# Moving the first projection of batches 1 to 3 into the first attention, half a tile at a time

## The reference

```
qkv    = x @ qkv_w.T                                  (q, k, v per head)
scores = alpha * tanh(q k^T / beta) + lam/2 * s s^T + lat
         s = tanh(x @ hex_w.T),  h = tanh(x @ q6_w.T),  lat[head] = h M[head] h^T / 6 * scale
out    = softmax(causal(scores)) @ v
```

## Time and profile before

| | us |
|---|---|
| median of 3 runs | 4202.61 (4201.70 to 4206.91) |
| the profiled execution | 4210.31 |
| its span | 4208.5 |
| PE / ACT / DVE / POOL busy in it | 3719.3 / 3380.6 / 2746.0 / 455.1 |
| mean granted TensorE clock | 0.974 |

### The profile page before, as it was taken

One profiled execution on the slowest core, in us unless ns is written; L12 is line 12 of the kernel. 1 busy time (PEld: TensorE's weight loads), 2 busy tenths in 40 slices (PEclk: granted clock), 3 DMA queues, 4 the chain that ended last, 5 costly groups with the idle time before them and its releaser, 6 DMA issues. The chain is left out here.

```text
span 4208.5 us, 61509 instructions
## 1 busy us (share of the span) xinstructions
PE 3719.3 (88%) x21948; PEld 1426.6 (34%) x21958; DVE 2746.0 (65%) x4740; ACT 3380.6 (80%) x2758; POOL 455.1 (11%) x407
## 2 busy tenths in 40 slices
PE   6969999998998999999997858759999999999687
PEld 2432322322332322232232644422222222222565
DVE  5647888778888777888877878952323233232688
ACT  2439999999999999999998113439999999999233
POOL 3530000000000000000000216730000000000232
PEclk9989999999999999999999989979999999999899
DMA  5861111111112111211110535652212222221331
GB/s 163 257 208 56 48 57 54 45 40 57 59 47 60 45 45 46 60 48 58 54 45 15 165 122 153 190 162 69 80 58 81 68 74 77 69 81 38 112 91 50
DMA packets 281330, 348.02 MB, mean 83 GB/s; under 512 B 39310, under 2 KB 214510, under 8 KB 280753
## 3 DMA queue, kind: packets, MB, share of 16 engines
q1 hardware_dynamic: 281012, 343.97, 27.2%
HBM read 215.56 MB, written 128.25 MB: 82 GB/s over the span
## 5 line engine op out<-in xcount | busy, mean ns | idle before, releaser
L842 DVE SCALAR_TENSOR_TENSOR att_prob<-att_tanh,alpha,ps 128x512 f32<-128x512 f32 x2176 | 1506.5, 740 | 410.4 <-ACT att_tanh L786 367.4
L726 PE MATMUL ps<-att_q,att_k 99*128 99x512 bf16 (+5 forms) x5120 | 1135.0, 351 | 114.1 <-DMA att_v<-v_ones 56.3
L755 PE MATMUL ps<-att_prob,att_v 128*32 128x512 f32 (+3 forms) x10240 | 1162.4, 540 | 2.0 <-ACT att_prob L795 1.9
L786 ACT ACTIVATE att_tanh<-ps,rbeta 128x2048 f32<-128x2048 f32 x544 | 1125.6, 2069 | 35.8 <-PE ps L726 35.8
L795 ACT ACTIVATE att_prob<-att_prob 128x2048 f32<-128x2048 f32 x544 | 1095.6, 2014 | 1.5 <-DVE att_prob L842 1.3
L792 ACT ACTIVATE att_prob<-ps 128x1024 f32<-128x1024 f32 x1088 | 1054.3, 1021 | 25.9 <-PE ps L726 10.0
L736 PE MATMUL ps<-att_f,att_g 75*128 75x512 bf16 (+3 forms) x2560 | 810.9, 354 | 133.1 <-DVE att_prob L842 121.3
L726 PEld LDWEIGHTS ps<-att_q,att_k 96*128 96x128 bf16 (+1 forms) x5120 | 399.4, 98 | 962.7 <-ACT att_prob L792 428.1
L831 DVE TENSOR_TENSOR att_prob<-att_prob,keep 128x512 f32<-128x512 f32 (+1 forms) x320 | 187.4, 586 | 580.3 <-ACT att_prob L792 579.1
L736 PEld LDWEIGHTS ps<-att_f,att_g 75*128 75x128 bf16 x2560 | 231.7, 97 | 927.6 <-DVE att_prob L842 906.8
L755 PEld LDWEIGHTS ps<-att_prob,att_v 128*32 128x32 f32 x10240 | 216.1, 108 | 347.9 <-ACT att_prob L792 141.6
(11 more groups left out here) (130 smaller groups left out, 2450.6 us busy)
## 6 DMA issues: line engine op xcount, KB each, us to landing
v_ones<-proj_vs SPq DMA_DIRECT2D x128, 256.0 KB, 3.3
att_v<-v_ones SPq DMA_DIRECT2D x128, 256.0 KB
att_k<-k_parts SPq DMA_DIRECT2D x128, 192.0 KB
att_q<-q_parts SPq DMA_DIRECT2D x128, 192.0 KB
att_k<-k_parts SPq DMA_DIRECT2D x128, 128.0 KB
att_q<-q_parts SPq DMA_DIRECT2D x128, 128.0 KB
o_t<-att_on SPq DMA_DIRECT2D x512, 32.0 KB, 1.7
post_o<-o_t SPq DMA_DIRECT2D x32, 512.0 KB, 5.1
```

The source lines that it names most:

```text
L726: mm = pe.matmul(ps[:, bank, col:col + w], keys, q_s[:, n % QU, h, q0:q0 + w], start=True, stop=True)
L755: mm = pe.matmul(ps[VW * h:VW * (h + 1), O0 + n % 2, q0:q0 + w], v_s[:, c % KU, kb % CB, h * VW:(h + 1) * VW], prob[:, S % R, h, col:col + ...
L786: th.done(act.activation(tanh_s[:, S % 2], ps[:, QK0:QK0 + HQ], ACT.Tanh, scale=kn["rbeta"][:, 0:1]))
L842: sc.done(dve.scalar_tensor_tensor(prob[:, S % R, h], tanh_s[:, S % 2, h], kn["alpha"][:, 0:1], ps[:, E0 + h % 2], ALU.mult, ALU.add))
```

## The change

`project_phase(0)` runs over the four groups of batch 0 only. The other twelve groups `X` are made inside `attend_phase(0)`, one per set in sets 0 to 11. A group is nine *units*: g, q0, q1, k0, k1, f0, f1 and two halves of v. A unit is two *halves* on PE (one for an f). `slots` names the 16 steps of a set behind which a half is put. The unit goes into bank 6 or 7, whichever is free between two query groups. DVE copies q, k, f and v units out in the step after (g goes through ACT's tanh), between the second and the third sum. POOL makes all three parts with four operations, and SP stores them. Normalising moves ahead of the first sum. SP's order in the attention is written out by step, with the waits for the stores of a batch (`projected`) ahead of the loads that need them. `row_max_phase` gets the missing tiles in its flagged branch, which isn't run in the profile.

```diff
+    kinds = tiles + [("v", 0), ("v", 1)]
+    NX = (B - 1) * GB if layer == 0 else 0
+    slots = {7: (0, 0), 8: (0, 1), 12: (1, 0), 13: (1, 1), 14: (2, 0), 15: (2, 1), 16: (3, 0), 17: (3, 1), 18: (4, 0), 19: (4, 1),
+             24: (5, 0), 25: (6, 0), 26: (7, 0), 27: (7, 1), 28: (8, 0), 29: (8, 1)}
+    bank_of = {u: O0 + (1 if 1 <= u <= 4 else 0) for u in range(NU)}
+    behind = {0: 0, 1: 1, 5: 2}
+    ahead = {2: 0, 3: 4, 0: 8}
...
 @block.sync
+            for n in range(QU):
+                load(n)
+                if layer == 0 and n == 0:
+                    for name, t in (("wq", wq_s), ("wk", wk_s), ("wv", wv_s), ("w12", w12_s)):
+                        sp.dma_start(t[:], w[name]).then_inc(w_in, 16)
+                    load_x(0)
+                    load_x(1)
+            for S in range(N + 8):
+                if 4 <= S < N + 4:
+                    it, s, *_ = at(S - 4)
+                    for g in ends[s]:
+                        n = it * GB + g
+                        if n + QU < NG:
+                            o_tr.wait(sp, n)
+                            b = (n + QU) // (GB * NHQ)
+                            if layer == 0 and b > 0 and (n + QU) // GB % NHQ == 0:
+                                projected((b - 1) * GB + (n + QU) % GB)
+                            load(n + QU)
+                if 5 <= S < N + 5 and unit_at(S - 5) is not None:
+                    store_unit(unit_at(S - 5))
+                if 7 <= S < N + 7:
+                    it, s, *_ = at(S - 7)
+                    for g in ends[s]:
+                        store_o(it * GB + g)
...
 @block.tensor
+            def project(j, half):
+                X, kind, m, tile, n, bank = unit(j)
+                if half == 0:
+                    if j == 0:
+                        pe.wait_ge(w_in, 64)
+                    if kind == "g":
+                        pe.wait_ge(x_in[X % 2], 16 * (X // 2 + 1))
+                    bg_ev.wait(pe, j - 1)
+                    if j % NU in behind:
+                        o_tr.wait(pe, X * GB + behind[j % NU])
+                if kind == "f":
+                    mm = pe.matmul(ps[0:n, bank], kn["Cq"][:].rearrange("p q e h -> p (q e h)")[:, m * n:(m + 1) * n], f12[:, X % 2], start=True, stop=True)
+                elif kind == "v":
+                    at_t = slice((2 * m + half) * P, (2 * m + half + 1) * P)
+                    for c in range(DC):
+                        mm = pe.matmul(ps[:, bank, half * D:(half + 1) * D], xt_s[:, X % 2, c, at_t], wv_s[:, c, :], start=c == 0, stop=c == DC - 1)
+                else:
+                    lhs = w12_s[:, half, :] if kind == "g" else (wq_s if kind == "q" else wk_s)[:, half, m * P:(m + 1) * P]
+                    mm = pe.matmul(ps[0:n, bank], lhs, xt_s[:, X % 2, half], start=half == 0, stop=half == 1)
+                if half == 1 or kind == "f":
+                    bg_ps.done(mm)
...
                 if layer == 0 and S < N:
                     extra(S, 2)
                     extra(S, 3)
+                if half_at(S):
+                    project(*half_at(S))
...
 @block.scalar
+                if S > 0 and unit_at(S - 1) is not None:
+                    feature(unit_at(S - 1))
                 if S > 0 and layer == 0:
                     sc.wait(act, (S - 1) * HQ + HQ - 1)
...
 @block.vector
+            dve.memset(vs[:], 1.0).then_inc(ones_set, 1)
+            def evict(j):
+                if kind == "v":
+                    bg_ps.wait(dve, j)
+                    v_out.wait(dve, m, X - 1)
+                    bg_ev.done(dve.tensor_copy(vs[:, m, :, :, 0:HD], ps[:, bank].rearrange("p (t h d) -> p t h d", t=2, h=H)))
+                elif kind != "g":
+                    bg_ps.wait(dve, j)
+                    low.wait(dve, tile - 2)
+                    bg_ev.done(dve.tensor_copy(raw[0:n, tile % 2], ps[0:n, bank]))
...
-                    if h == 2:
+                    if h == 0:
                         normalise(due, 1)
+                    if h == 2 and S > 0 and unit_at(S - 1) is not None:
+                        evict(unit_at(S - 1))
                     th.wait(dve, S)
                     ex.wait(dve, S * HQ + h)
...
 @block.gpsimd
+                for j in range(NX * NU):
+                    bg_ev.wait(pool, j)
+                    parts_out.wait(pool, u, tile // 2 - 1)
+                    hi.done(pool.tensor_copy(parts[0:n, u, 0], src))
+                    rest.done(pool.tensor_tensor(rem[0:n], src, parts[0:n, u, 0], ALU.subtract))
+                    mid.done(pool.tensor_copy(parts[0:n, u, 1], rem[0:n]))
+                    low.done(pool.tensor_tensor(parts[0:n, u, 2], rem[0:n], parts[0:n, u, 1], ALU.subtract))
...
-        project_phase(nc, kn, 0, {"wq": chunked(a["wq0"]), "wk": chunked(a["wk0"]), "wv": chunked(a["wv0"]), "w12": chunked(a["w12"]), "xt": chunked(a["x0_t"])}, None)
+        project_phase(nc, kn, 0, w0, None, NB=1)
```

More of the change, by code:

```diff
@@ L628, in attend_phase, with half_at, unit_at, unit @@
     QK0, E0, O0 = 0, 4, 6
+    tiles = [("g", 0), ("q", 0), ("q", 1), ("k", 0), ("k", 1), ("f", 0), ("f", 1)]
+    NTL = len(tiles)
+    kinds = tiles + [("v", 0), ("v", 1)]
+    NU = len(kinds)
+    NX = (B - 1) * GB if layer == 0 else 0
[4 more added lines that the diff above has]
+    ahead = {2: 0, 3: 4, 0: 8}
+    def half_at(S):
+        it, s = divmod(S, NST)
+        if it >= NX or s not in slots:
+            return None
+        return it * NU + slots[s][0], slots[s][1]
+    def unit_at(S):
+        found = half_at(S)
+        return found[0] if found and (found[1] == 1 or unit(found[0])[1] == "f") else None
+    def unit(j):
+        X, u = divmod(j, NU)
+        kind, m = kinds[u]
+        return X, kind, m, X * NTL + u, {"q": P, "k": P, "f": 96, "g": NF, "v": P}[kind], bank_of[u]
     SR, FR = (QROWS, FROWS + 3) if layer == 0 else (QROWS + 3, 0)
@@ L753, in weigh @@
                         o_tr.wait(pe, n - 2)
+                        X = it - 1 if g == 0 else it
+                        if g in ahead and 0 <= X < NX:
+                            bg_ev.wait(pe, X * NU + ahead[g])
                     for h in range(HQ):
@@ L779, in _, with feature @@
                 c.start(act)
+            def feature(j):
+                X, kind, m, tile, n, bank = unit(j)
+                if kind == "g":
+                    bg_ps.wait(act, j)
+                    if X >= 2:
+                        low.wait(act, tile - 2 * NTL)
+                    bg_ev.done(act.activation(f12[:, X % 2], ps[0:NF, bank], ACT.Tanh))
             for S in range(N + 1):
@@ L798, in _ @@
         def _(dve):
-            for c in (sc, o_tr, o_rc, o_mul, o_n, kept):
+            for c in (sc, o_tr, o_rc, o_mul, o_n, kept) + ((bg_ev,) if layer == 0 else ()):
                 c.start(dve)
@@ L876, in row_max_phase @@
         flagged = ph.sem("flagged")
+        tiles = [("g", 0), ("q", 0), ("q", 1), ("k", 0), ("k", 1), ("f", 0), ("f", 1)] if layer == 0 else []
+        NTL = len(tiles)
+        NTB = GB * NTL
+        rows_of = {"q": P, "k": P, "f": 96, "g": NF}
+        if layer == 0:
+            w_in, x_in, tile_ps, feat, split, tile_out = (ph.sem(n) for n in ("w_in", "x_in", "tile_ps", "feat", "split", "tile_out"))
+            wq_s, wk_s = (ph.sb(n, [P, DC, D]) for n in ("wq", "wk"))
+            w12_s, f12 = ph.sb("w12", [P, DC, NF]), ph.sb("f12", [NF, TG])
+            xt_s = ph.sb("xt", [P, DC, TG])
+            tparts = ph.sb("tparts", [P, 3, TG], BF16)
+            trem = ph.sb("trem", [P, TG])
         ps = kn["ps"]
@@ L893, in _ @@
             with sp.If(wide == 1):
+                if layer == 0:
+                    for name, t in (("wq", wq_s), ("wk", wk_s), ("w12", w12_s)):
+                        sp.dma_start(t[:], w[name]).then_inc(w_in, 16)
+                    with sp.Fori(0, B - 1) as b:
+                        for gq in range(GB):
+                            J0 = b * NTB + gq * NTL
+                            wait(sp, split, J0 * 4 + 1, ph.passed)
+                            sp.dma_start(xt_s[:], w["xt"][:, :, bass.ds((b + 1) * T + gq * TG, TG)]).then_inc(x_in, 16)
+                            for t, (kind, m) in enumerate(tiles):
+                                n, per = rows_of[kind], {"g": NF, "f": H * NF}.get(kind, D)
+                                row = (b + 1) * (GB * per) + gq * per + m * n
+                                wait(sp, split, (J0 + t) * 4 + 5, ph.passed)
+                                sp.dma_start(kn[f"{kind}_d"][:, bass.ds(row, n), :].rearrange("k r t -> r k t"), tparts[0:n]).then_inc(tile_out, 16)
+                    wait(sp, tile_out, (B - 1) * NTB * 16 + 16, ph.passed)
                 with sp.Fori(0, B) as b:
@@ L935, in _ @@
                 if layer == 0:
+                    with act.Fori(0, B - 1) as b:
+                        for gq in range(GB):
+                            act.wait_ge(tile_ps, b * NTB + gq * NTL + 1)
```

(1 more changed line is left out.)

123 lines of the change are left out of this document (105 added, 18 removed).

## The result

| | before | after |
|---|---|---|
| median of 8 runs each, us | 4204.74 | 4179.94 (4172.19 to 4194.02) |
| profiled execution / its span | 4210.31 / 4208.5 | 4194.02 / 4192.2 |
| first tanh of the attention | 306.83 | 133.05 |
| last tanh of the attention | 2296.74 | 2280.03 |

The ratio is 0.9946, interval [0.9934, 0.9959]: 25 us faster, where 78 were forecast.

A forecast was written before the change was run, and what follows sets the result against it. First projection bound by PE, first attention by ACT. Removed groups −173.0, slots +94, normalising −2, start +3.2 give −78 us: 4202.6 to 4125 us; range 4085 to 4165, also given as 4085 to 4168.

The forecast's parts named there:

- the loop: Attention slots: path from extra 0 through DVE's sums, half and weigh to the next extra 0 exceeds the 3.65 us step.
- slots, 12 sets: Attention sets carrying halves: 7.8 us more per set, +94 us over 12 sets.
- normalising ahead of the sums: Attention: normalising uses DVE's idle time before the first sum, saving some 0.14 us per set, −2 us.
- What a slot costs PE: Attention slots: 2.75 + 0.90 us of work just fits 3.65, but the order doesn't; 9.2 us per set.
- A: Slot whose half brings no new wait, ten per set: 4.04 us, 0.39 over the step.
- B: Slot whose half waits for DVE to empty the unit before, six per set: 4.43 us, 0.78 over the step.
- What is absorbed: Slack at the starts of the three slot runs and at the fourth sum takes 1.8 us per set, leaving 7.4.
- Rival 2: Attention slots: each half pays another 0.15 us, 29 us, plus 7 at the start: 4161; within the forecast's 0.81.
- The start theory: Attention start: loads of weights and x on SP delay load(1), for which PE waits: +3.2 us.
- Rival 1: Attention: PE has room for all halves, only tanh and start costs remain: −167 us, 4036 us; chance 0.10.
- rival 3: Attention sums: POOL's four operations per tile hold DVE up, about 4360 us at 0.70 us each; chance 0.05.
- rival 4: SP in the attention: late stores delay a batch's loads and ACT runs dry; no change or a loss, chance 0.04.

The follow-up runs named there:

- run with padding: Changed kernel with the f matmuls contracting over 128 rows, zero-padded, instead of 12: 4162.13 us, ratio 0.9899.
- PE's halves alone: Changed kernel with all 16 groups projected ahead again; PE's 192 halves still run but unread, without evictions, feature tanh, POOL or stores: 4301.17 us, ratio 1.0228.
- kernel with early evictions: Changed kernel with a unit's eviction moved from between the second and third sum to ahead of the first: 4139.96 us, ratio 0.9843.
- the later loads: Changed kernel with both edits, padding, and loads of weights and x behind the attention's third load instead of its first: 4066.60 us, ratio 0.9676.
- both edits: Changed kernel with the half between extras 2 and 3 and eviction ahead of the first sum: 4085.79 us without one 10237.79 us execution, ratio 0.9725.

## Why the prediction was wrong

The direction was right and so was the mechanism of the loop, the size was not: −25 us for −78. 4180 stands outside the range, whose upper end the prediction gives once as 4165 and once as 4168. The clock was no part of the mechanism forecast. By its steps, in the profiled execution:

| term | predicted | measured |
|---|---|---|
| removed groups (first tanh 306.83 to 133.05) | −173.0 | −173.8 |
| slots, 12 sets | +94 | +128 (135.0 − 124.3 = 10.7 per set) |
| clock drops in sets 1 to 11 | none | +25 (what these sets take beyond 135.0) |
| start of the attention | +3.2 | +4.0 (set 0: 8.0 over 135.0, before 4.0 over 124.3) |
| normalising ahead of the sums | −2 | −0.4 on sets 12 to 14 (124.1 to 124.2 for 124.3); in the slotted sets part of the 10.7 |

This is −16, the difference of the two spans (4192.2 − 4208.5). The median of the change lies lower than its profiled execution. The run with padding is 18 us under that median; in it the drops are gone, and each set is 0.2 us shorter (2.4 us in all). So the drops cost about 15 us in a median execution and 25 in the profiled one.

**"What a slot costs PE" failed first.** The loop is there, but two of its terms were taken from a neighbour that was a little too good. In A, 4.04 was forecast and is 4.17: DVE takes extra 0 up 0.14 after its end instead of 0.09 (1157.04 + 0.38 to 1157.56; I had used the signal from ACT), and a half holds PE for 0.96 instead of 0.90, since the projection's average has no neighbours of another kind. In B, 4.43 was forecast and is 4.61: the half that starts after a wait holds PE for 1.06. The copy is 0.68 (0.69 taken) and its signal 0.06. Ten times 0.13 and six times 0.18 are 2.4 us per set, 29 us in all.

**"What is absorbed" failed next.** It let the slack at the fourth sum swallow an eviction. But behind the last slot of a run the copy still stands between the sums, the fourth sum comes late, and exp waits for it. That is steps 21 and 31, 0.42 and 0.53 too long, 0.95 us per set and 11 in all. With the copy ahead of the first sum they take 3.67. The smaller terms nearly cancel: steps 17 to 20, beside steps with masks, take 0.6 more than plain ones where 0.25 was taken; the tanh of the features was to cost 0.38, and step 9 takes 4.15 with it against 4.10 without it (PE's halves alone); the starts of the runs absorb 2.1 instead of 1.8. Added up this is 3.1 us per set over the forecast of 7.8, for 10.9 over the 124.1 of a set without slots.

**The clock was missing altogether.** I argued that the granted clock was 1.00 in both stages and did not ask what a stretch with both kinds of work would get. The padded run shows that the drops come with the f matmuls over twelve rows, 15 to 25 us for which the sum had no term. What in them brings the drops is open.

**The range failed with it.** Rival 2, "the loop is dearer", had the right side and 29 us for it; the loop alone would have landed at its end (4125 + 34 = 4159), and the padded run, with the loop and without the drops, measures 4162. The drops put the kernel past 4168.

**What held.** The projection ends and the attention starts where they were forecast; the slots are longer, and besides them only steps 21 and 31 and the steps with a drop; B stands behind the six slots named. The transfers and stores cost next to nothing after the start: the kernel with early evictions has all of them and takes 131.9 per set, the one without stores 131.6. The start theory (loads of weights ahead of load(1)) is shown by the later loads. Rival 1 (room for everything) is excluded by the run with PE's halves alone, rival 3 (GpSimd) by the sums beside POOL, 742 ns against 744, rival 4 (late stores) by the first sets of batches 1 to 3, which in the padded run take 134.8, 134.8 and 124.1 us like their neighbours.

## What to carry to other kernels

When work is moved into the idle time of an in-order engine, don't add up its free time: write down the loop through all engines from an instruction to its successor one step later, and look where the new piece stands in it. The same 192 pieces cost 128 us behind the last wait of the step, and 18 (12 × 1.5) between two waits that were there anyway, with the evictions in an idle stretch of their engine, the f matmuls padded, and away from steps that are full. A wait that exists is a place to put work. A place behind the last wait was none here, though the engine looked idle there on average.

## What the hardware showed that was not expected

In this attention a float32 matmul over twelve rows is dearer than the same one padded to 128 rows with zeros. Its weights are loaded late (1.34 us from extra to extra instead of 1.08), and in this mix the granted clock falls to 1.2 GHz behind it, which cost 15 to 25 us. Padding took both away; whether the two hang together was not tried. All five kernels with twelve rows have drops in the attention (nine, four, six, one and four), the three padded ones none. The same two matmuls do no harm to the clock in the old projection (1.00), nor much where the steps are shorter (one drop in twelve sets with both edits).

How long a float32 half holds PE differs with its place: 0.86 us between two extras (611.62 to 612.48), 0.96 between an extra and weigh, 1.06 behind a wait. POOL's four operations per tile take 0.61, 1.16, 0.61 and 1.16 us, and no sum is longer beside them.
